# A four-block vision network on one core: results in PSUM placed by a table of banks instead of by fixed names, with new orders of the steps

## The chip, the core and the metric

The kernel runs on one core of a Trainium2 chip. A core has TensorE (PE in the profile, its weight loads PEld), VectorE (DVE), ScalarE (ACT), GpSimd (POOL) and SyncE (SP), each with its own queue of instructions that runs in order; they wait for each other through semaphores. TensorE writes its products into PSUM, which has eight banks of 128 partitions x 512 float32; VectorE and ScalarE read them there. The metric is the time of one execution on the device in microseconds (us), less is better.

## What is computed

Input x is (4, 256, 32, 32) float32: four images, 256 channels, 1024 pixels. Four residual blocks, each on the group-normalised x (32 groups of 8 channels), follow each other:

```python
x = x + _L0_conv_ref(_gn(x), ...)   
x = x + _L1_conv_ref(_gn(x), ...)
x = x + _L2_conv_ref(_gn(x), ...)
x = x + _L3_conv_ref(_gn(x), ...)
...
# L0
q = _conv1x1(x, q_w, q_b)
x_ds = lax.conv_general_dilated(x, ds_w, window_strides=(sr, sr), ...)
kv = _conv1x1(layernormed x_ds, kv_w, kv_b)
attn = jax.nn.softmax(jnp.einsum('bcm,bcn->bmn', q, k), axis=-1)
out = jnp.einsum('bmn,bcn->bcm', attn, v)
out = _conv1x1(out, proj_w, proj_b)
...
# L1
xd, z = jnp.split(xz, 2, axis=-1)
xc = jax.nn.silu(3x3 depthwise convolution of xd + cb)
delta = jax.nn.softplus(...)
h = a * h + bu          
y = layernorm(h * c + Ds * u)
out = layernorm((y * silu(z)) @ op_w, times gate and skip) @ proj_w.T + proj_b
...
# L2
attn = jnp.einsum('bnhi,bnhj->bhij', q, k) * scale
attn = jax.nn.softmax(jnp.clip(attn, -50.0, 50.0), axis=-1)
out = proj of einsum('bhij,bnhj->bhin', attn, v)
...
# L3
s = jax.nn.relu(score from the channel means, two small layers)
pools = max pooling with windows (1, 3, 5, 7, 9, 11, 13)
return frac_b * b_out + frac_s * s_out + x
```

The listing is condensed: words stand for longer expressions. L0 is attention with 8 heads of 32 channels, 1024 queries and 256 keys per image. L1 is a scan over the 1024 pixels in four directions, one for each 64 channels. L2 is attention between channels (32 x 32 for each head). L3 mixes two neighbouring sizes of max pooling for each channel.

## The kernel before

Images are counted from 0 to 3 here. The work is cut into streams, one letter each, and every stream runs over the images in turn: F (first norm, down-sampling, queries, keys and values), A (scores, softmax, weighted sums), C (first projection, second norm, layer norm, 3x3 convolution), B (gate, delta, scan, its norms, second projection), D (third norm, transposes to pixel rows, Gram matrix, channel attention, its output), M (fourth norm, scores and max pooling of images 0 and 1, summed on VectorE) and L (the same for images 2 and 3, summed on TensorE with weights on a diagonal). A stream is a Python generator for each engine; each `yield` ends a step. A string for each engine, `PE_ORDER`, `ACT_ORDER`, `DVE_ORDER`, `POOL_ORDER` and `SP_ORDER`, says whose steps come next: `F11 A33` is eleven steps of F, then 33 of A. So the order of work on each engine is fixed by hand-held tables, and nothing is decided on the chip but the waiting.

Each step has a label (`s0_0`, `mT0`, `pv0_0`, `proj1_0_0`), and raises its stream's semaphore; a reader waits for the label's number. Labels that matter below:

- A: `s{h}_{j}` (L1626) is the score of head h for a pair of query tiles; VectorE's `mx{h}_{j}` (L1071) takes the maxima of the rows. `mT{g}` (L1634) transposes the maxima, VectorE splits them in two and SyncE copies them below the queries. `st{g}_{kt}_{j}` (L1646) is the transposed score with the maximum subtracted, and ScalarE's exponential `p{g}_{kt}_{j}` (L549) reads it. `pv{g}_{kt}` (L1661) multiplies with the values and with ones; ScalarE's logarithm and exponential (L559, L562) make the inverse sums, VectorE's L1088 multiplies.
- F: `ds` (L1586), `q` (L1552 with WQ), `k` (L1606), `vT` (L1613). The keys are split in a high half (KH, ScalarE) and a low half (KL, VectorE, L1058), and SyncE (L410) and ScalarE's queue (L538) copy query and key halves into the stacks QST and KST that the scores read.
- C: `proj0` (L1552 with GA), `gn1` (L1545), `sums1` (L1573), `xd` (L1680), the convolution of nine taps.
- B: `z`, `v`, `yc` and `yv` (all L1694, four blocks of 64 x 64), `fc1`, `fc2` (the gate's small layers), `B` and `C` (L1725), `op` (L1760), `sums2` (L1573), `proj1` (L1552 with PS and WP); VectorE's `r2` (L1110) reads `proj1` and multiplies it with the norm that ScalarE has to make first (L592).
- D: `xnT` (L1770), `gram` (L1782), `rows`, `T1` (L1803), `A` (L1812), `PAT` (L1824), `WE` (L1832), `be`, `cst` (L1507), `R` (L1853), `out` (L1552 with XR and BUF).

The eight banks have names, and each kind of result has its own: `aD0`, `aD1` for scores, transposed maxima, weighted sums, first projection and half of the convolution; `aA0`, `aA1` for transposed scores, sums of C and the other half; `bA0`, `bA1` for most of B and D; `pp0`, `pp1` for F, the small layers, C chunks and the rest. Steps of one kind use the two banks by turns. Before TensorE writes into a bank, `take` lets it wait for the last reader that was noted for it:

```python
def take(self, e, slot, reader):
    if slot in self.last:
        e.wait_ge(*self.last[slot])
    self.last[slot] = reader
```

TensorE runs in order, so whatever stands behind a step that waits for a bank waits too.

## Time and profile before

| | |
|---|---|
| median of 3 runs | 857.36 us (853.52 to 858.54) |
| profiled execution, its own time | 855.84 us |
| its span, first to last instruction | 853.2 us |
| TensorE busy | 83% of the span |
| VectorE busy | 66% |
| ScalarE busy | 50% |
| GpSimd busy | 4% |
| mean granted TensorE clock | 0.895 of full |
| DMA, mean | 31 GB/s |

All later times are microseconds from the start of the span of this one execution. A row of a group of instructions gives line, engine, operation, what it writes <- what it reads with the buffers' numbers left out, shapes, the count, then the busy time of all and the mean ns of one, and after the last bar the engine's idle time just before such instructions and what ended it.
### The profile page before, as it was taken

What the parts mean: (1) busy time and instruction counts of PE and PEld (TensorE: products, weight loads), DVE (VectorE), ACT (ScalarE), POOL (GpSimd) and SP (SyncE); (2) the same over time, 40 slices, a digit from 0 to 9 for tenths busy, and PEclk for the clock granted to TensorE, in tenths of its full rate; (3) what the DMA queues carried; (4) which work ended last, traced back from release to release, by engine and by line L of the source; (5) the groups of instructions that cost most, each with busy time, mean ns of one, the idle gap of its engine ahead of it and who ended that gap; (6) DMA issues with size and microseconds to landing.
All of it is one profiled execution on the core that took longest, in us unless ns stands there. A gap on an engine that the chain in (4) does not pass through costs nothing.

```text
span 853.2 us, 9378 instructions
## 1 busy us (share of the span) xinstructions
PE 704.7 (83%) x3384; PEld 318.8 (37%) x3384; DVE 561.6 (66%) x1057; ACT 424.3 (50%) x703; POOL 32.8 (4%) x26
## 2 busy tenths in 40 slices
PE   4848986898988899999799887798597887889685
PEld 4514332243323356443333443133234452355331
DVE  3563438226829632775678888968996858876586
ACT  1202555379576557656665637576756335521211
POOL 3300002000001000000020000000200000000000
PEclk9956998799999999989889898999788669999889
DMA  7330131000131000003200000011000010000101
GB/s 265 101 93 1 50 85 58 2 1 0 51 89 54 1 2 1 1 2 85 58 1 2 1 1 2 0 56 44 0 1 1 0 50 1 0 0 1 50 0 49
DMA packets 15056, 26.87 MB, mean 31 GB/s; under 512 B 3314, under 2 KB 7058, under 8 KB 14883
## 3 DMA queue, kind: packets, MB, share of 16 engines
q1 hardware_dynamic: 11712, 22.80, 8.7%
q10 hardware_dynamic: 3298, 3.48, 1.4%
q8 instruction: 27, 0.44, 0.2%
q14 instruction: 19, 0.15, 0.1%
HBM read 14.09 MB, written 4.19 MB: 21 GB/s over the span
## 4 chain that ended last, share of the span: by engine, by line
PE 56%; DVE 22%; ACT 14%; issue 5%; SPq 1%; POOL 1%; DMA 0%; ACTq 0%; DVEq 0%; POOLq 0%
PE aD L1661 6%; PE aA L1680 4%; DVE NEGMAX L1071 4%; PE bA L1552 4%; PE aD L1680 4%; PE pp L1586 4%; PE bA L1694 3%; PE bA L1782 3%; PE aA L1646 2%; ACT PT L549 2%; PE aD L1552 2%; DVE PA_ L1398 2%; DVE HB L1393 2%; PE aD L1626 2%; PE aA L1573 2%
## 5 line engine op out<-in xcount | busy, mean ns | idle before, releaser
L549 ACT ACTIVATE PT<-aA 128x512 f32<-128x512 f32 x128 | 70.1, 593 | 85.0 <-PE aA L1646 84.5
L1071 DVE TENSOR_REDUCE NEGMAX<-aD 128x2 f32<-128x512 f32 x128 | 82.0, 684 | 24.3 <-PE aD L1626 23.0
L1626 PE MATMUL aD<-KST,QST 96*128 96x256 f16 x256 | 53.0, 312 | 25.6 <-DVE NEGMAX L1071 18.0
L1646 PE MATMUL aA<-QST,KST 98*128 98x512 f16 x128 | 45.3, 411 | 16.0 <-ACT PT L549 11.5
L1398 DVE TENSOR_TENSOR PA_<-HB 128x1024 f32<-128x1024 f32 x40 | 49.0, 1226 | 5.0 <-PE aD L1950 4.0
L1393 DVE TENSOR_TENSOR HB<-PA_ 128x1024 f32<-128x1024 f32 x40 | 48.9, 1221 | 0.6
L1626 PEld LDWEIGHTS aD<-KST,QST 96*128 96x128 f16 x256 | 19.5, 104 | 65.2 <-DVE NEGMAX L1071 38.7
L1680 PE MATMUL aA<-XNP,WTAP 64*64 64x512 f32 x288 | 37.2, 673 | 6.2 <-issue 5.7
L1552 PE MATMUL bA<-PS,WP 128*128 128x512 f32 x64 | 33.5, 663 | 9.8 <-DVE PS L1110 9.8
L880 POOL TENSOR_TENSOR GA<-GA,PT 128x1024 f32<-128x1024 f32 x8 | 19.1, 2408 | 560.3 <-ACT PT L577 560.3
L1950 PE MATMUL aD<-PA_,PT 128*128 128x512 f32 x56 | 31.2, 685 | 9.2 <-DVE PA_ L1398 5.2
L1661 PE MATMUL aD<-PT,VT 128*32 128x512 f32 x256 | 38.0, 669 | 0.8 <-DVE GV_F L975 0.8
L1661 PE MATMUL aD<-PT,ONES 128*32 128x512 f32 x256 | 35.8, 634 | 0.0
L1088 DVE TENSOR_TENSOR GA<-GA,aD 128x512 f32<-128x512 f32 x16 | 11.0, 686 | 35.9 <-ACT GA L562 30.1
L1950 PE MATMUL aA<-PA_,PT 128*128 128x512 f32 x56 | 29.5, 651 | 6.2 <-ACT PT L807 3.9
L1782 PE MATMUL bA<-SQX 128*128 128x257 f32 x128 | 32.4, 414 | 2.5 <-ACT G L623 2.5
L1646 PEld LDWEIGHTS aA<-QST,KST 98*128 98x128 f16 x128 | 11.0, 100 | 60.3 <-ACT PT L549 33.7
L1552 PE MATMUL aD<-GA,WP 128*128 128x512 f32 x64 | 29.3, 601 | 3.1 <-DVE GA L1088 2.6
L1680 PE MATMUL aD<-XNP,WTAP 64*64 64x512 f32 x288 | 31.7, 589 | 0.0
L1552 PE MATMUL pp<-XF,WQ 128*128 128x512 f32 x64 | 30.3, 600 | 1.5 <-DVE QL L1050 1.5
L1407 DVE SCALAR_TENSOR_TENSOR ACC<-PA_,COEF,ACC 128x1024 f32<-128x1024 f32 x24 | 30.8, 1281 | 0.5
L1586 PE MATMUL pp<-XF,WDS 128*128 128x256 f32 x128 | 30.6, 397 | 0.0
(303 smaller groups left out, 1374.8 us busy)
## 6 DMA issues: line engine op xcount, KB each, us to landing
XF<-in_x SPq DMA_DIRECT2D x8, 512.0 KB, 3.8
QST<-QH SPq DMA_DIRECT2D x32, 128.0 KB, 2.7
XR<-in_x SPq DMA_DIRECT2D x4, 1024.0 KB, 4.9
...
```

Of the source, the lines that this page charges most:

```text
L549: e.activation(PROB[:, 4 * kt + j, :], SLOT[f"aA{j % 2}"][:, :], ACT.Exp)\
L1071: e.tensor_reduce(NEGMAX[:, h, 2 * j:2 * j + 2], SLOT[f"aD{j % 2}"][:, :].rearrange("p (t k) -> p t k", t=2), AX.X, ALU.max, negate=True). ...
L1393: e.tensor_tensor(HB[:, 1:1 + H, :], PA4[:, cc, 1:1 + H, 0:W], PA4[:, cc, 1:1 + H, 2:2 + W], ALU.max)\
L1398: e.tensor_tensor(PA4[:, cc, 1:1 + H, 1:1 + W], HB[:, 0:H, :], HB[:, 2:2 + H, :], ALU.max)\
L1552: mm = e.matmul(s[:, :], w(cc), src[:, cc, hs(half)], start=(cc == 0), stop=(cc == CC - 1))
L1586: mm = e.matmul(s[:, m * NK:(m + 1) * NK], WDS[:, cc, n % 4, m * P:(m + 1) * P], src, start=(n == 0), stop=(n == 4 * CC - 1))
L1626: mm = e.matmul(s[:, t * NK:(t + 1) * NK], QST[0:96, h, qt * P:(qt + 1) * P], KST[0:96, h, :], start=True, stop=True)
L1646: e.matmul(s[:, :], KST[0:98, h, kt * P:(kt + 1) * P], QST[0:98, h, hs(g % 2)], start=True, stop=True)\
L1661: mm = e.matmul(SLOT[slot][HD * j:HD * j + HD, :], w, PROB[:, 4 * kt + j, :], start=(kt == 0), stop=(kt == 1))
L1680: mm = e.matmul(banks[gi][64 * half:64 * half + 64, :], WTAP[rows, cc, tap(2 * cc + gi, dy, dx), :], XNP[rows, cc, dy + 16 * half:dy + 16 ...
L1782: mm = e.matmul(s[:, 0:C + 1], XNT[:, t, m * P:(m + 1) * P], XNT[:, t, :], start=(t == 0), stop=(t == QT - 1))
L1950: mm = e.matmul(SLOT[("aA", "aD")[cc] + str(half)][:, :], DG[:, cc, k, :], PA4[:, cc, 1 + 16 * half:17 + 16 * half, 1:1 + W], start=(k == ...
```

## The change

Two things change; the computation does not.

First, the eight banks are now one list, `PSB[0]` to `PSB[7]`. For each stream a table of the source, `BANKS_A` and so on, gives the bank of each step of each image, in the order of the labels; `-` stands for a step that takes no new bank (it adds to an earlier one). A step with two results has two digits. Maker and readers look up the bank of the same label:

```diff
+class Banks:
+    def __init__(self, tensors, text, steps, first=0):
+        self.tensors, self.words, self.first = tensors, text.split(), first
+        labels = steps.split()
+        self.index, self.count = {x: n for n, x in enumerate(labels)}, len(labels)
+    def at(self, b, label, n=0):
+        return int(self.words[(b - self.first) * self.count + self.index[label]][n])
...
+BANKS_A = """
+4 5 6 7 0 1 2 3 4 5 6 7 0 1 2 3 4 6 7 0 1 2 3 4 5 6 7 0 1 2 3 4 6 57 0 1 2 3 - 0 4 1 6 2 3 7 5 4 1 6
...
-        SLOT = {n: ctx.enter_context(nc.psum_tensor(n, [P, HALF], f32))
-                for n in ("aA0", "aA1", "aD0", "aD1", "bA0", "bA1", "pp0", "pp1")}
+        PSB = [ctx.enter_context(nc.psum_tensor(f"PSB{n}", [P, HALF], f32)) for n in range(8)]
...
-            def take(b, slot, engine, label):
-
-                slots.take(e, slot, engine.at(b, label))
-                return SLOT[slot]
+            def take(st, b, step, engine, label, n=0):
+
+                k = BANKS[st].at(b, step, n)
+                slots.take(e, k, engine.at(b, label))
+                return PSB[k]
...
-                    s = take(b, f"aD{j % 2}", dve_a, f"mx{h}_{j}")
+                    s = take("A", b, f"s{h}_{j}", dve_a, f"mx{h}_{j}")
...
-                    s = take(b, f"aA{j % 2}", act_a, f"p{g}_{kt}_{j}")
+                    s = take("A", b, f"st{g}_{kt}_{j}", act_a, f"p{g}_{kt}_{j}")
```

All other uses of a bank are edited in the same way. In the setup the two small folds now lie in banks of their own, and the weighted sums take their two banks in the other order. The wait for a bank's last reader remains, but the reader is now that of the step that had the bank before by the table.

Second, the orders of TensorE, ScalarE and VectorE are new (GpSimd's and SyncE's are as they were):

```diff
 PE_ORDER = """
-F11 A33 F1 A3 F1 A3 F1 A8 F1 A3 F1 A6 F1 A2 F1 A7 F1 A5 F1 A4 C4 A4 C1 A4 C2 A2 F1 A7 C2 A2 B1 F1 B1
...
+F11 A17 F1 A30 F1 A6 F1 A9 F1 A11 F1 A1 F2 C4 F2 C1 A10 C2 A7 B1 A16 F1 A9 C2 B2 A3 B1 A2 F1 B3 A5
...
```

What stands on TensorE at three places, before and after. The first is where image 2's scores begin (L1626 before, L1690 after). PS,WP is image 0's or image 1's second projection, XNP,WTAP the convolution, XF,WDS the down-sampling, MAT,G the transposes of D. Before:

```order
L1626 MATMUL aD<-KST,QST 128x256 x4
L1552 MATMUL bA<-PS,WP 128x512 x4
L1626 MATMUL aD<-KST,QST 128x256 x4
L1545 MATMUL pp<-MV_F,MAT 128x4
L1552 MATMUL bA<-PS,WP 128x512 x4
L1680 MATMUL aA<-XNP,WTAP 64x512 x36
L1545 MATMUL pp<-MV_D,MAT 128x4
L1626 MATMUL aD<-KST,QST 128x256 x4
L1586 MATMUL pp<-XF,WDS 128x256 x16
```

After (XDS,WK and WV,XDS are image 2's keys and values, XNP,IPZ and U,WD four-block products of B, SQX Gram of D, MAT,NEGMAX the transposed maxima):

```order
L1670 MATMUL PSB<-XDS,WK 128x256 x4
L1758 MATMUL PSB<-XNP,IPZ 64x512 x4
L1677 MATMUL PSB<-WV,XDS 128x256 x4
L1758 MATMUL PSB<-XNP,IPZ 64x512 x4
L1776 MATMUL PSB<-GAPX,W1S 16x1 x2
L1782 MATMUL PSB<-HM,SMALL 128x1 x2
L1690 MATMUL PSB<-KST,QST 128x256 x32
L1847 MATMUL PSB<-SQX 128x257 x8
L1758 MATMUL PSB<-U,WD 64x512 x4
L1698 MATMUL PSB<-MAT,NEGMAX 32x128
```

The 16 pairs of scores of heads 0 to 3 (32 products) stood in pieces among other streams, and now stand in one row.

The second place is image 0's second projection, with the banks' numbers. Before:

```order
L1552 MATMUL bA0<-PS,WP1 128x512 x2
L1552 MATMUL bA1<-PS,WP1 128x512 x2
L1626 MATMUL aD1<-KST,QST 128x256 x2
L1626 MATMUL aD0<-KST,QST 128x256 x2
L1545 MATMUL pp0<-MV_F,MAT 128x4
L1552 MATMUL bA0<-PS,WP1 128x512 x2
L1552 MATMUL bA1<-PS,WP1 128x512 x2
L1680 MATMUL aA0<-XNP,WTAP 64x512 x2
```

After:

```order
L1616 MATMUL PSB3<-PS,WP1 128x512 x2
L1616 MATMUL PSB6<-PS,WP1 128x512 x2
L1616 MATMUL PSB1<-PS,WP1 128x512 x2
L1616 MATMUL PSB7<-PS,WP1 128x512 x2
L1744 MATMUL PSB2<-XNP,WTAP 64x512 x2
```

The four blocks used two banks twice and now use four, with nothing between them.

The third place is TensorE after image 3's last weighted sum. GA,WP is image 3's first projection. Before (U,MAT is a centring of B, MAT,T the rows R of D, XR,BUF the output of D):

```order
L1694 MATMUL bA<-U,MAT 64x512 x4
L1853 MATMUL pp<-MAT,T 32x128 x32
L1552 MATMUL bA<-XR,BUF 128x512 x2
L1694 MATMUL pp<-SQX,MAT 64x512 x4
L1552 MATMUL bA<-XR,BUF 128x512 x6
L1694 MATMUL pp<-SQX,MAT 64x512 x4
L1552 MATMUL aD<-GA,WP 128x512 x2
L1545 MATMUL pp<-MV_M,MAT 128x4
```

After (WP,ABD is PAT and T,W2V is WE of image 1; MV_C is `gn1`, the group norm of image 3's C):

```order
L1758 MATMUL PSB<-U,MAT 64x512 x4
L1889 MATMUL PSB<-WP,ABD 128x256 x2
L1758 MATMUL PSB<-U,MAT 64x512 x4
L1616 MATMUL PSB<-GA,WP 128x512 x2
L1897 MATMUL PSB<-T,W2V 128x256 x4
L1758 MATMUL PSB<-SQX,MAT 64x512 x4
L1616 MATMUL PSB<-GA,WP 128x512 x2
L1574 MATMUL PSB<-COL,T 128x1 x4
L1574 MATMUL PSB<-GM_D,BUF 128x1 x4
```

```order
L1616 MATMUL PSB<-PS,WP 128x512 x8
L1616 MATMUL PSB<-GA,WP 128x512 x2
L1609 MATMUL PSB<-MV_M,MAT 128x4
L1609 MATMUL PSB<-MV_C,MAT 128x4
```

One more centring and PAT, WE, be and cst of image 1 now stand behind the last weighted sum, and all of image 2's second projection stands ahead of image 3's last projection block and group norm. Before, two of its four blocks stood behind that norm.

## Rows read from the trace of the kernel before

**Rows 1.** The page: its first line, and busy time by engine
```profile
span 853.2 us, 9378 instructions
PE 704.7 (83%) x3384; PEld 318.8 (37%) x3384; DVE 561.6 (66%) x1057; ACT 424.3 (50%) x703; POOL 32.8 (4%) x26
```

**Rows 2.** Stretches: length, busy PE PEld DVE ACT POOL, clock, DMA, GB/s
```profile
417.20:559.80 142.60, 119.85 (x619) 48.58 (x618) 121.90 (x207) 84.41 (x132) 4.68 (x2) 0.88 0.00 1
559.80:803.00 243.20, 199.09 (x912) 98.57 (x910) 184.80 (x355) 116.34 (x192) 5.12 (x2) 0.87 0.05 18
803.00:853.30 50.30, 31.43 (x66) 12.24 (x66) 36.38 (x57) 7.45 (x22) 0.00 (x0) 0.85 0.05 21
```

**Rows 3.** TensorE's groups by line and shape, whole span
```profile
L1626 PE MATMUL aD<-KST,QST 96*128 96x256 f16 x256 | 53.0, 312 | 25.6 <-DVE NEGMAX L1071 18.0 <-DMA KST<-KL 5.0 <-DVE XR L1098 1.1
L1646 PE MATMUL aA<-QST,KST 98*128 98x512 f16 x128 | 45.3, 411 | 16.0 <-ACT PT L549 11.5 <-DMA QST<-ML 3.4
L1552 PE MATMUL bA<-PS,WP 128*128 128x512 f32 x64 | 33.5, 663 | 9.8 <-DVE PS L1110 9.8
L1782 PE MATMUL bA<-SQX 128*128 128x257 f32 x128 | 32.4, 414 | 2.5 <-ACT G L623 2.5
L1552 PE MATMUL pp<-XF,WQ 128*128 128x512 f32 x64 | 30.3, 600 | 1.5 <-DVE QL L1050 1.5
L1725 PE MATMUL bA<-U,XB 128*128 128x512 f32 x32 | 20.8, 775 | 3.4 <-DVE AOK L1245 1.7 <-DVE SQX L1162 1.0 <-ACT T L699 0.7
L1725 PE MATMUL pp<-U,XC 128*128 128x512 f32 x32 | 16.6, 632 | 2.3 <-DVE PS L1174 1.3 <-DVE QL L1050 1.0
L1694 PE MATMUL bA<-U,MAT 64*64 64x512 f32 x64 | 15.5, 859 | 1.2 <-DVE SQX L1162 1.2
L1634 PE MATMUL aD<-MAT,NEGMAX 128*32 128x128 f32 x8 | 2.5, 317 | 6.8 <-DVE NEGMAX L1071 6.3 <-ACT U L613 0.5
```

**Rows 4.** Timeline of image 0's second projection: start, length, engine, instruction
```profile
280.60 1.98 PE L1552 MATMUL bA<-PS,WP 128*128 128x512 f32 x4 [1.38 <-DVE PS L1110]
285.03 3.58 PE L1552 MATMUL bA<-PS,WP 128*128 128x512 f32 x4 [2.45 <-DVE PS L1110]
...
279.86 0.69 DVE L1110 TENSOR_TENSOR PS<-bA,PS 128x512 f32<-128x512 f32 x1 [2.00 <-ACT PS L592]
```

**Rows 5.** Timeline, TensorE at image 0's first and last row of scores
```profile
47.56 1.03 PE L1626 MATMUL aD<-KST,QST 96*128 96x256 f16 x4 [4.95 <-DMA KST<-KL]
...
57.70 1.02 PE L1626 MATMUL aD<-KST,QST 96*128 96x256 f16 x3
```

**Rows 6.** Groups of VectorE and ScalarE: the scores' readers
```profile
L1071 DVE TENSOR_REDUCE NEGMAX<-aD 128x2 f32<-128x512 f32 x128 | 82.0, 684 | 24.3 <-PE aD L1626 23.0
L549 ACT ACTIVATE PT<-aA 128x512 f32<-128x512 f32 x128 | 70.1, 593 | 85.0 <-PE aA L1646 84.5
```

**Rows 7.** Two stretches of image 0's attention; weighted sums at either clock
```profile
47.50:77.00 29.50, 21.21 (x75) 5.62 (x75) 21.00 (x40) 4.85 (x10) 0.00 (x0) 0.50 0.13 42
77.00:120.70 43.70, 41.63 (x233) 19.63 (x225) 13.80 (x26) 21.78 (x41) 0.00 (x0) 1.00 0.12 35
...
76.07 1.54 PE L1661 MATMUL aD<-PT,ONES 128*32 128x512 f32 x8
...
86.37 1.04 PE L1661 MATMUL aD<-PT,ONES 128*32 128x512 f32 x8
```

**Rows 8.** Timeline, SyncE's issues of query copies; DMA issues of key copies
```profile
35.62 6.10 SPq L410 DMA_DIRECT2D QST<-QH  x8
...
KST<-KL SPq DMA_DIRECT2D x16, 32.0 KB, 1.9
```

**Rows 9.** TensorE's groups by shape: small steps of D
```profile
L1832 PE MATMUL bA<-T,W2V 128*128 128x256 f32 x32 | 9.6, 453 | 1.5 <-ACT SQX L670 1.2 <-ACT GT L638 0.3
L1507 PE MATMUL bA<-GM_D,BUF 128*128 128x1 f32 x32 | 6.3, 319 | 2.4 <-ACT BUF L715 2.4
L1824 PE MATMUL bA<-WP,ABD 128*128 128x256 f32 x16 | 4.2, 384 | 1.7 <-DVE ABD L1276 1.7
```

More of the change, by code:

```diff
@@ L230, in __init__, with take @@
         self.last = {}
-    def take(self, e, slot, reader):
-        if slot in self.last:
-            e.wait_ge(*self.last[slot])
-        self.last[slot] = reader
+    def take(self, e, bank, reader):
+        if bank in self.last:
+            e.wait_ge(*self.last[bank])
+        self.last[bank] = reader
 def program(nc, x, cols, mats, wq, wk, wv, wds, wp0, small16, w1s, ipx, ipz, cw, xpr, dtp, xb, xc, opw,
@@ L1563, in sums @@
             def sums(b, l, src, ready):
[L1565 removed]
+                pe, act, dve, st, squares, _, _ = NORM["C" if l == 1 else "B"]
                 e.wait_ge(*dve.at(b, ready))
@@ L1568, in sums @@
                 for half in range(2):
-                    s = take(b, f"{banks}{half}", dve, f"ln_var{l}" if half else f"ln_var{l}_0")
+                    s = take(st, b, f"sums{l}_{half}", dve, f"ln_var{l}" if half else f"ln_var{l}_0")
                     for cc in range(CC):
@@ L1673, in convolve @@
                 e.wait_ge(*act_c.at(b, "xn1"))
-                banks = [take(b, ("aA", "aD")[cc] + str(gi), act_c, f"xd{cc}_{gi}_1") for gi in range(2)]
+                banks = [take("C", b, f"xd{cc}_{gi}", act_c, f"xd{cc}_{gi}_1") for gi in range(2)]
                 for n in range(TAPS):
@@ L1707, in small_mlp @@
                 pe, dve, hidden = (last_steps(b)[0], last_steps(b)[2], HM3) if at else (pe_b, dve_b, HM1)
-                s = take(b, "pp0", dve, f"hm{l}")
+                st = last(b) if at else "B"
+                s = take(st, b, steps[0], dve, f"hm{l}")
                 e.wait_ge(*sources)
@@ L1713, in small_mlp @@
                 yield
-                s = take(b, "pp1", dve, "sc0" if at else "gate_in")
+                s = take(st, b, steps[1], dve, "sc0" if at else "gate_in")
                 e.wait_ge(*dve.at(b, f"hm{l}"))
@@ L1787, in channel_scores @@
             def channel_scores(b):
-                s = take(b, "bA0", dve_d, "srow")
+                s = take("D", b, "rows", dve_d, "srow")
                 e.wait_ge(*dve_d.at(b, "gram1"))
@@ L1819, in attended @@
             def attended(b):
-                s = take(b, "bA1", act_d, "pat")
+                s = take("D", b, "PAT", act_d, "pat")
                 e.wait_ge(*dve_d.at(b, "abd3"))
```

327 lines of the change are left out of this document (184 added, 143 removed), and 3 rows, old and new, of the table BANKS_B.

## The prediction

> **What bounds the kernel now.** I read the page first, then the table of stretches, then the groups of instructions by shape, and last the timeline of two places. The page shows TensorE busy for 704.7 of 853.2 us, VectorE for 561.6 and ScalarE for 424.3 [rows 1]. So no engine is full; TensorE comes nearest, and its 148.5 us of idle time (853.2 - 704.7) are what an order and a choice of banks can work on.
>
> The stretches [rows 2] are cut at the first score and the last weighted sum of each image. In the last attention's stretch, 417.2 to 559.8 us, TensorE is busy for 119.85 of 142.6 us and VectorE for 121.90. From 559.8 us on, only the rest of image 1, the chains of images 2 and 3 are left: TensorE is busy for 199.1 of 243.2 us and VectorE for 184.8, and the last 50.3 us are the pooling of image 3 alone.
>
> The groups [rows 3] say who ended TensorE's idle time. I sort them by asking whether the instruction waited for its data or for a bank that somebody still had to read. Waits for a bank: scores 18.0 (L1626, on the maxima), transposed scores 11.5 (L1646, on the exponentials), second projection 9.8 (L1552, on L1110), and smaller ones: B chunks 3.4 and C chunks 2.3 (L1725), Gram 2.5 (L1782), queries 1.5 (L1552), centring 1.2 (L1694), together 10.9. The sum is 50.2 us, a third of the idle time. The rest is waits for data, as 6.3 at the transposed maxima (L1634), and would stay.
>
> **What the change removes.** The eight names of banks that each belonged to one kind of result become one pool. The maker of the score of pair j no longer needs the reader of pair j-2. Four terms follow.
>
> Second projection. At 280.60 and 285.03 us TensorE had stood for 1.38 and 2.45 us, because bA0 and bA1 were full: VectorE's L1110 had itself waited 2.00 us for ScalarE and read the first of them only at 279.86 [rows 4]. The changed table gives the four blocks four banks (3, 6, 1, 7 for image 0), so TensorE writes them all and goes on to the convolution. I take all of the 9.8 us, bounds 0 and 9.8.
>
> Small bank waits, 10.9. Counted in the tables, 328 of the 612 uses of a bank came four steps or fewer after its last use, and 48 now do. I take all 10.9, bounds 0 and 10.9.
>
> Scores, 18.0. Here the reader can be the pace and not the bank. In image 0 the 16 pairs run from 47.56 to 58.72 us, 0.70 each, and one maximum takes 0.684 [rows 5, 6]: eight banks can't make that faster. In later images VectorE was late with other work, and there a longer queue helps. I take half, 9.0, bounds 0 and 18.0.
>
> Transposed scores, 11.5. The same with ScalarE, whose exponential takes 0.593 us [rows 6]. Half, 5.8, bounds 0 and 11.5.
>
> Removed in all: 9.8 + 10.9 + 9.0 + 5.8 = 35.5 us.
>
> **What the change adds.** The new order puts the attention into blocks. All 16 pairs of images 2 and 3 stand in a row on TensorE, then one Gram product and one four-block product, then the transposed maxima.
>
> Runs of scores. One maximum is 0.684 us, so 16 take 10.9 us. At the lower clock two pairs, four records, take 1.03 us on TensorE [rows 5]; at the full clock I put 0.3 for a pair, 4.8 for 16. The first eight pairs find banks free; the other eight come at VectorE's pace, 8 x 0.684 = 5.5 against 2.4: a wait of 3 us per image, 9 for three. The second batch (eight transposed scores, eight pairs) has 5.5 us of maxima and 4.7 of exponentials against about 4.8 of TensorE: 1 us per image, 3. Of these 12 us, 6.3 stand already in the wait of L1634 [rows 3], since what ends that wait is the same maxima. Added: 5.7, bounds 0 and 12.
>
> Weighted sums of pairs 1 to 3 now have little else between them. ScalarE needs 8 x 0.593 and about 1.2 for logarithm and reciprocal, 5.9 us a pair; TensorE needs four sets of eight records of at most 1.04 us at full clock [rows 7], 4.2, plus eight transposed scores, some 2. They nearly balance. One third of a us for each of nine: 3, bounds 0 and 9.
>
> Keys. In image 0 the first score waited until 47.56 us for the copies of the low key halves, with TensorE idle for 4.95 [rows 5]. SyncE had started at 35.62, as soon as the last query half was there, and took 6.10 us to issue the eight query copies; a key copy takes 1.9 more to land [rows 8]. So 11.9 us lie between the last query and the first score. SyncE's own order is unchanged, and so is GpSimd's. But TensorE's k of image 1 now stands right before that image's scores, with only vT and one small product between, and ScalarE squares image 0's residual before it copies these keys. From image 1's last query product to its first score TensorE has four projection blocks, k and vT, about 8 us (2 each for the blocks at 33.5 / 16 [rows 3]), against the 11.9. I take 4 us open. In images 2 and 3 the queries are long done, and vT, two four-block products (at most 1.9 each) and two small layers lie behind k: 1 us each. Added: 6, bounds 0 and 12.
>
> Clock. From 47.5 to 77.0 us, where TensorE did little else than scores, its granted clock was 0.50, the lower level; from 77.0 it was 1.00, after dense work [rows 7]. At the lower level eight records of the weighted sums took 1.54 us (76.07), at the full one 1.04 (86.37). So a third of the time at the lower level is lost; a lull with the stretch behind it, some 4 us, costs 1.3. Six new lulls (two in each of images 1 to 3): 8, bounds 0 and 16.
>
> The Trainium skill speaks against this change here: its page "TensorE: Matmul & The Clock Gate", section "A second HAM failure mode: psum-queue depth-cycling", tells of a kernel that cycled through banks, idled briefly between groups and so fell back and forth between the levels. The trace shows both levels in this kernel, but not yet for that cause. The page "Perfetto Trace Analysis", section "Matmul Optimizations", advises the use of all eight banks and would let one expect only the gain, 853.2 - 35.5.
>
> Added in all: 5.7 + 3 + 6 + 8 = 22.7. The same matmuls, activations and copies run. The work before image 3's last weighted sum hardly changes: some small steps of image 1 and a centring of image 2 move behind it.
>
> **The sum.** Against the profiled execution: 853.2 - 35.5 + 22.7 = 840.4 us of span. That execution took 855.84 us, 2.6 more than its span, so 843.0. The median of the runs is 857.4, 1.5 above the profiled one; that is a fifth of a per cent and I leave it out.
>
> **Rivals.** *The waits only move.* The readers are the pace nearly everywhere: the halves of scores and transposed scores come back as nothing (-14.8) and the rest stays: 35.5 - 14.8 - 22.7 = -2.0, so 858. For it speaks image 0, where 0.70 us a pair stands against 0.684. Against it speaks that ScalarE's exponentials waited 84.5 us for TensorE in all [rows 6], so ScalarE is seldom the pace.
>
> *The full gain.* Later images' scores were held by banks alone and the lulls are filled: 50.2 recovered and 12 added give 815 of span, 818 in all.
>
> *Slower: image 3's tail starts later.* From its last weighted sum to the end lie 293.4 us in which the chain projection, norm, convolution, scan, channel attention, pooling of image 3 runs once. The new order puts on TensorE ahead of its group norm: one centring of image 2 (15.5 / 8 = 1.9), PAT, WE and cst of image 1 (4.2 / 4 = 1.1, 9.6 / 4 = 2.4, 6.3 / 4 = 1.6), and two more blocks of the second projection (33.5 / 16 = 2.1 each) [rows 3, 9]: 11.2 us. If the last weighted sum still comes at 560 and the gains of images 0 to 2 vanish in the blocks, the end moves by these 11.2 us: 867. It decides if that sum comes later than about 549. For it: TensorE's work before that point shrinks by only those first steps. Against it: in the tail TensorE is idle for 44 us (243.2 - 199.1), so part is absorbed, and 7.0 of the 11.2 have left the stretch before.
>
> *Slower: the clock.* If each attention block of images 1 to 3 runs as image 0 did until 77 us, 29.5 us at the lower level with TensorE busy for 21.2 [rows 7], a third of that is lost in each: 7.1, and with the same lost again in the second half of the block, whose loops are as sparse, 14.1; 42 for three instead of the 8 above: 877. It ends on the slow side from 10.3 us a block on. The skill's page just named would favour this one.
>
> **How the numbers follow.** Forecast (825 to 849): 0.48. Full gain (below 825): 0.11. Waits only move (849 to 866): 0.20. Later tail: 0.12. Clock: 0.09. A measurement of this kernel can tell about 1% from no change, some 8.6 us either way of 857.4. Faster is the first two, 0.59; same 0.20; slower 0.21. The range reaches from a little below the full gain, 815, to the later tail with a small margin, 870. It leaves out about 1 in 10 on each side. The likeliest case's own range is 825 to 849.
>
> **What would show it.** L1626's successor should lose most of its idle time on maxima outside the runs, and the second projection all of its 9.8. The first score of image 1 should wait for a key copy. Of the half-clock stretches there should be new ones in the attention blocks of images 1 to 3. VectorE's and ScalarE's busy times should be unchanged. The last weighted sum of image 3 should end near 549 us and the first of image 3's pooling products near 791. The forecast is wrong if TensorE's idle time doesn't fall below 140 us, or if the tail is longer than 300.

## The result and the profile after

The changed kernel takes 783.2 us at the median (781.5 to 783.7), beside 857.3 us for the kernel before. The ratio is 0.9139, with a 95% interval of 0.9112 to 0.9165: faster by 74 us, where the forecast was 14 and its range ended at 815. In a later set of runs the same kernel took 783.7 (ratio 0.9141, interval 0.9121 to 0.9161).

The page of the changed kernel, the same lines as in [rows 1]:

```profile
span 779.7 us, 9375 instructions
...
PE 664.2 (85%) x3384; PEld 313.0 (40%) x3384; DVE 555.0 (71%) x1057; ACT 418.3 (54%) x703; POOL 34.6 (4%) x26
```

The span lost 73.5 us. TensorE's idle time fell by 33.0, from 148.5 to 115.5 (779.7 - 664.2). Its busy time fell by 40.5, from 704.7, although it runs the same 3384 matmuls. VectorE's and ScalarE's fell by only 7 and 6. Any explanation has to find both halves.

TensorE's groups by line and shape in the changed kernel, as [rows 3]: busy us, mean ns of one, and the idle time before them with what ended it. The old lines 1626, 1646, 1552, 1634 and 1694 are now 1690, 1710, 1616, 1698 and 1758; the line on which VectorE reads the scores went from 1071 to 1130.

```profile
L1690 PE MATMUL PSB<-KST,QST 96*128 96x256 f16 x256 | 41.7, 310 | 12.6 <-DMA KST<-KL 7.3 <-ACT PT L607 1.3 <-DVE GA L1147 1.1
...
L1710 PE MATMUL PSB<-QST,KST 98*128 98x512 f16 x128 | 37.4, 408 | 4.7 <-ACT PT L607 1.8 <-DVE PS L1235 1.4 <-DVE AOK L1306 0.4
...
L1616 PE MATMUL PSB<-PS,WP 128*128 128x512 f32 x64 | 28.7, 599 | 0.0
...
L1758 PE MATMUL PSB<-U,MAT 64*64 64x512 f32 x64 | 15.5, 859 | 7.1 <-DVE U L1239 7.1
```

The second projection waits no more, and the scores' wait for the maxima, 18.0 us in [rows 3], is not among the first three. But look at the busy column too: the scores fell from 53.0 to 41.7 us with the mean of one record nearly the same (312 and 310). The group's busy time is the time covered by its records. Records that follow each other closely overlap; the first after a pause overlaps with nothing before it.

The changed kernel in stretches, cut where the first score of image 0 starts and where each image's last weighted sum ends, then the whole. The columns are those of [rows 2].

```profile
47.20:103.80 56.60, 48.10 (x277) 23.10 (x277) 30.64 (x60) 23.13 (x46) 0.00 (x0) 0.87 0.13 41
103.80:208.90 105.10, 88.72 (x515) 37.49 (x516) 56.41 (x102) 65.12 (x104) 4.64 (x2) 0.92 0.15 40
208.90:343.20 134.30, 128.19 (x671) 54.41 (x671) 89.37 (x180) 94.07 (x154) 4.69 (x2) 0.97 0.09 24
343.20:490.50 147.30, 142.42 (x802) 65.75 (x805) 128.19 (x242) 100.30 (x162) 6.95 (x2) 0.99 0.09 22
490.50:779.70 289.20, 226.76 (x1012) 109.72 (x1012) 230.83 (x427) 127.64 (x222) 4.66 (x2) 0.89 0.05 19
```

From 208.9 to 490.5 us TensorE idles for only 11.0 of 281.6 us, at a granted clock of 0.97 and 0.99. The last weighted sum of image 3 ends at 490.5, not at 559.8 as before: 69 of the 73.5 us are won by then. The tail is 289.2 us long, before 293.4.

The stretches at the lower of the two clock levels are fewer. These are the stretches table's closing rows for all of them together, first of the kernel before (23 stretches), then of the changed kernel (17).

```profile
sum 178.80, PE 137.59 PEld 60.63 DVE 127.81 ACT 77.40 POOL 4.65; mean PE 5.98 PEld 2.64 DVE 5.56 ACT 3.37 POOL 0.20
```

```profile
sum 110.40, PE 71.60 PEld 37.55 DVE 85.36 ACT 45.83 POOL 4.36; mean PE 4.21 PEld 2.21 DVE 5.02 ACT 2.70 POOL 0.26
```

TensorE was busy at the lower level for 137.6 us before and for 71.6 after. At that level a third of the time is lost (1.54 us against 1.04, [rows 7]), so by this estimate the clock stands for (137.6 - 71.6) / 3 = 22 of the 40.5 us of busy time.

### The profile page after: what moved, and what is told of

Read it like the earlier page. It is cut to its first block, busy times and chain, and to the rows that moved or that the text cites. A ratio compares the mean times of both kernels' runs of the same rounds, so it can differ in the third digit from the quotient of the medians.

```text
span 779.7 us, 9375 instructions
## 1 busy us (share of the span) xinstructions
PE 664.2 (85%) x3384; PEld 313.0 (40%) x3384; DVE 555.0 (71%) x1057; ACT 418.3 (54%) x703; POOL 34.6 (4%) x26
## 4 chain that ended last, share of the span: by engine, by line
PE 51%; DVE 24%; ACT 15%; issue 6%; SPq 1%; POOL 1%; DMA 1%; ACTq 0%; DVEq 0%; POOLq 0%
PE PSB L1616 11%; PE PSB L1744 6%; PE PSB L1725 5%; PE PSB L1650 3%; PE PSB L1758 3%; PE PSB L1637 3%; DVE PA_ L1459 3%; DVE NEGMAX L1130 3%; PE PSB L2015 3%; DVE HB L1454 3%; PE PSB L1710 2%; PE PSB L1690 2%; PE PSB L1825 2%; PE PSB L1574 1%; SPq L468 1%
## 5 line engine op out<-in xcount | busy, mean ns | idle before, releaser
L1130 DVE TENSOR_REDUCE NEGMAX<-PSB 128x2 f32<-128x512 f32 x128 | 78.6, 680 | 15.0 <-PE PSB L1690 14.7
L607 ACT ACTIVATE PT<-PSB 128x512 f32<-128x512 f32 x128 | 65.7, 604 | 31.1 <-PE PSB L1710 31.0
L2015 PE MATMUL PSB<-PA_,PT 128*128 128x512 f32 x112 | 58.6, 658 | 15.8 <-DVE PA_ L1459 7.0
L1744 PE MATMUL PSB<-XNP,WTAP 64*64 64x512 f32 x576 | 63.4, 591 | 0.0
L1690 PE MATMUL PSB<-KST,QST 96*128 96x256 f16 x256 | 41.7, 310 | 12.6 <-DMA KST<-KL 7.3
L1710 PE MATMUL PSB<-QST,KST 98*128 98x512 f16 x128 | 37.4, 408 | 4.7 <-ACT PT L607 1.8
L1690 PEld LDWEIGHTS PSB<-KST,QST 96*128 96x128 f16 x256 | 24.4, 110 | 32.3 <-ACT PT L607 8.2
L1725 PE MATMUL PSB<-PT,VT 128*32 128x512 f32 x256 | 34.0, 603 | 0.6 <-DVE NEGMAX L1130 0.3
L1725 PE MATMUL PSB<-PT,ONES 128*32 128x512 f32 x256 | 33.4, 592 | 0.0
L1650 PE MATMUL PSB<-XF,WDS 128*128 128x256 f32 x128 | 31.6, 406 | 0.2 <-DVE NEGMAX L1130 0.2
L1616 PE MATMUL PSB<-GA,WP 128*128 128x512 f32 x64 | 30.0, 605 | 0.0
L1847 PE MATMUL PSB<-SQX 128*128 128x257 f32 x128 | 29.6, 386 | 0.4 <-DVE NEGMAX L1130 0.4
L1616 PE MATMUL PSB<-PS,WP 128*128 128x512 f32 x64 | 28.7, 599 | 0.0
```

Source lines behind the costliest of these rows:

```text
L607: e.activation(PROB[:, 4 * kt + j, :], bank("A", b, f"st{g}_{kt}_{j}")[:, :], ACT.Exp)\
L1130: e.tensor_reduce(NEGMAX[:, h, 2 * j:2 * j + 2], bank("A", b, f"s{h}_{j}")[:, :].rearrange("p (t k) -> p t k", t=2), AX.X, ALU.max, negate ...
L1616: mm = e.matmul(s[:, :], w(cc), src[:, cc, hs(half)], start=(cc == 0), stop=(cc == CC - 1))
L1650: mm = e.matmul(s[:, m * NK:(m + 1) * NK], WDS[:, cc, n % 4, m * P:(m + 1) * P], src, start=(n == 0), stop=(n == 4 * CC - 1))
L1690: mm = e.matmul(s[:, t * NK:(t + 1) * NK], QST[0:96, h, qt * P:(qt + 1) * P], KST[0:96, h, :], start=True, stop=True)
L1710: e.matmul(s[:, :], KST[0:98, h, kt * P:(kt + 1) * P], QST[0:98, h, hs(g % 2)], start=True, stop=True)\
```

## Experiments

There are two things in the change, the free banks and the order, and 17 runs look at them. Times are medians; each set of runs had the kernel before beside it on the same chip (855.7 to 857.4), and the ratios are to that.

### Banks alone, a smaller pool, two banks for one result, another table

The first kernel has the orders of before, and a table in which each result takes the bank that was read longest ago in the trace of before:

```diff
 BANKS_A = """
-4 5 6 7 0 1 2 3 4 5 6 7 0 1 2 3 4 6 7 0 1 2 3 4 5 6 7 0 1 2 3 4 6 57 0 1 2 3 - 0 4 1 6 2 3 7 5 4 1 6
+4 5 6 7 0 1 2 3 4 5 6 7 0 1 2 3 4 5 6 7 0 1 2 3 4 5 6 7 0 1 2 3 4 67 0 1 3 4 - 0 1 3 4 2 7 6 0 3 4 2
...
 PE_ORDER = """
-F11 A17 F1 A30 F1 A6 F1 A9 F1 A11 F1 A1 F2 C4 F2 C1 A10 C2 A7 B1 A16 F1 A9 C2 B2 A3 B1 A2 F1 B3 A5
+F11 A33 F1 A3 F1 A3 F1 A8 F1 A3 F1 A6 F1 A2 F1 A7 F1 A5 F1 A4 C4 A4 C1 A4 C2 A2 F1 A7 C2 A2 B1 F1 B1
...
```

> The orders of steps of all engines are those of the kernel before; only the banks are free: each result gets, in TensorE's order, the bank that had been read longest ago in the trace of before. My new theory: most of the 74 us come from the order, which needs eight banks to run at all; then banks alone give what the prediction's terms on banks say at most, 20 to 35 us (about 825 to 837), with TensorE's idle time down by about as much and its clock (0.895) and busy time (705) nearly as before. Rival A, banks alone give the whole gain: within 10 us of 783. Rival B, the readers are the pace: above 848.

Measured: 826.4 us, ratio 0.9651 (0.9620 to 0.9682). So the banks alone give 29 us, and the order gives 43 on top of free banks. The time is neither rival's. ("Pieces" below are stretches in which TensorE is busy without a pause.) The page and the first waits of TensorE (line, what it waited for, us in total, times, longest):

```profile
span 823.6 us, 9375 instructions
...
PE 681.8 (83%) x3384; PEld 325.0 (39%) x3384; DVE 558.7 (68%) x1057; ACT 421.4 (51%) x703; POOL 32.7 (4%) x26
```

```profile
PE PSB L1698 <- DVE NEGMAX L1130: 17.2, 6, 7.0
PE PSB L1637 <- issue: 12.2, 8, 4.2
PE PSB L1609 <- DVE MV_F L1006: 11.2, 1, 11.2
PE PSB L1744 <- issue: 8.8, 2, 5.5
...
PE PSB L1710 <- ACT PT L607: 1.7, 4, 0.9
```

Here my expectation was wrong in kind, though right in size. I had expected the idle time to fall by about the gain. It fell by 6.7, from 148.5 to 141.8. Bank waits, sorted as the prediction sorted them, are down from 50.2 to about 12, but waits for data have taken their place: TensorE now stands 17.2 us at the transposed maxima, 6.3 before [rows 3], because the 16 maxima ahead of them are VectorE's pace. The 12.2 and 8.8 us that the profile puts down to "issue" (an engine that waits for nothing shown) are of that kind too: each of these ten steps starts 0.1 to 0.2 us after ScalarE has finished what it reads (those at 131.39 and 599.69 us, for example, after 131.29 and 599.59). The waits put down to "issue" are 21.0 us here, 9.8 before and 2.4 in the changed kernel. The other 22.9 us of the span's gain are busy time. I counted TensorE's pauses in both traces: 184 separate busy pieces before, 96 with free banks. At the lower level TensorE was busy for 119.0 us instead of 137.6, a third of which is 6.2 us. 16.7 us are left, and 88 restarts fewer, 0.19 us each: what a pause costs beyond its idle time, if the whole rest is put on it. The other traces bear this out roughly. A straight-line fit of busy time over the 17 traces without fillers (fillers come below) gives 0.17 us for each piece and 0.42 us, not a third, for each us busy at the lower level, and misses no trace by more than 2.5 us. In the groups, the scores went from 53.0 to 40.5 us:

```profile
L1690 PE MATMUL PSB<-KST,QST 96*128 96x256 f16 x256 | 40.5, 300 | 5.3 <-DMA KST<-KL 4.4 <-ACT PT L607 0.5 <-DVE NEGMAX L1130 0.2
```

The next three keep the changed order. One uses only banks 0 to 6. One gives the four blocks of each second projection two banks in turn:

```diff
 BANKS_B = """
-21 63 4 5 60 53 7 5 4 2 6 4 0 2 53 07 56 02 6 2 3 6 2 0 3 6 1 7 05 02 5 3 73 40 0 5 3 7 4 7 7 3 75
-40 72 16 7 4 1 6 4 3 1 6 2 5 40 47 0 2 24 57 3 7 0 3 7 5 0 7 35 40 32 60 6 0 5 4 0 5 3 4 2 0 34 20 5
+21 63 4 5 60 53 7 5 4 2 6 4 0 2 53 07 56 02 6 2 3 6 2 0 3 6 3 6 05 02 5 3 73 40 0 5 3 7 4 7 7 3 75
+40 72 16 7 4 1 6 4 3 1 6 1 6 40 47 0 2 24 57 3 7 0 3 7 5 0 7 35 40 32 60 6 0 5 4 0 5 3 4 3 4 34 20 5
...
```

The third has the table by last reading. The changed table starts as in the line with the minus, that with seven banks and that by last reading as in the two with a plus:

```diff
 BANKS_B = """
-21 63 4 5 60 53 7 5 4 2 6 4 0 2 53 07 56 02 6 2 3 6 2 0 3 6 1 7 05 02 5 3 73 40 0 5 3 7 4 7 7 3 75
+24 46 1 3 10 54 6 3 5 2 1 3 4 0 21 50 31 20 2 6 2 1 0 2 1 5 4 0 15 35 1 1 32 54 6 0 5 1 3 0 2 2 50
...
+26 21 5 5 50 74 2 7 1 3 5 2 7 6 43 70 45 76 5 6 3 5 6 7 3 5 1 0 74 76 4 3 05 23 0 5 4 7 2 4 4 3 41
...
```

> The order of the changed kernel with bank 7 never used: every result has one of seven banks. By a rough count 93 results would find their bank still full, for 42 us in sum, many of them beside other waits. My theory (the order keeps TensorE several results ahead of its readers, and its long busy stretches are what holds the clock up): 15 to 40 us slower than the changed kernel (798 to 825), idle time of TensorE up by 10 to 25 and its busy time up by 3 to 10 with a lower clock. Rival (the queue's depth does not matter beyond a few banks): within 8 us of 783.

Measured: 795.0 us, ratio 0.9279 (0.9253 to 0.9305), 12 us above the changed kernel: idle time 121.4, up 5.9, busy time 673.6, up 9.4. That is between my 15 to 40 and the rival's 8. The depth counts, less than I thought, and more of it shows as busy time than as idle time.

> The changed kernel, only the last two of the four blocks of each second projection take the banks of the first two again. The prediction's term says that this pair of waits was worth 9.8 us for four images, so 790 to 793. Rival (the wait is hidden, since VectorE is the pace there and TensorE is ahead): within 3 us of 783.

Measured: 793.4 us, ratio 0.9273 (0.9243 to 0.9302), 10 us above by the medians and 11.5 by the ratios. The prediction's term for this wait, 9.8, is about its price under this order:

```profile
L1616 PE MATMUL PSB<-PS,WP 128*128 128x512 f32 x64 | 35.1, 701 | 11.4 <-DVE PS L1169 11.4
```

The group shows 11.4 us of waiting and 6.4 more of busy time (28.7 with free banks), 17.8 in all, of which 10 to 12 reach the end.

> The order of the changed kernel, its table replaced by another one over the same eight banks, in which each result takes the bank that was read longest ago in the trace of the changed kernel. If only the number of banks counts: within 3 us of 783. If the table itself was worth something beyond that: 5 to 15 us slower.

Measured: 779.4 us, ratio 0.9092 (0.9070 to 0.9113), and in another set of runs 778.2, 0.9081 (0.9062 to 0.9100) beside 0.9141 (0.9121 to 0.9161) for the changed kernel. The plain rule is 4 to 5 us faster than the table of the change, which neither of my two cases had: the table itself brings nothing beyond its order.

The remaining corner, the changed order with the fixed banks of before, was not run, because its waits close a circle: TensorE would wait for a bank whose reader stands in its own engine's queue behind something that TensorE has yet to make. So the new order is not only helped by free banks: it can't run on the old ones.

### One kind of result freed under the old order

Here only the words of one kind change, to a bank that stands empty at that time in the trace of before; all others keep what they had. The scores of image 2 as an example (its first 25 words: sixteen pairs, the transposed maxima, eight transposed scores):

```diff
-2 3 2 3 2 3 2 3 2 3 2 3 2 3 2 3 2 0 1 0 1 0 1 0 1
+0 1 7 3 4 5 2 3 6 2 1 7 3 2 0 1 2 0 1 0 1 0 1 0 1
```

> Order of before and its fixed banks for everything but the scores: 98 of the 128 scores go to a bank other than their two, wherever one of the eight is empty at that time in the trace of before. The prediction's term for the scores was half of their 18.0 us of idle time, 9.0, so 848. Theory: a pause costs more than the idle time that the rows show, since the pair after it starts with an empty pipeline (L1626 was busy for 53.0 us in before and its successor for 40.5 with all banks free), so 10 to 18 us: 839 to 847, busy time of the scores below 46. Rival: the waits move to the transposed scores and maxima, 852 to 858.

Measured: 852.6 us, ratio 0.9956 (0.9938 to 0.9973), 3.7 us. The rival holds, with its range. The scores' wait for maxima fell from 18.0 to 4.4 us and their busy time from 53.0 to 42.6, but the waits are handed on:

```profile
L1690 PE MATMUL PSB<-KST,QST 96*128 96x256 f16 x256 | 42.6, 309 | 9.9 <-DMA KST<-KL 5.4 <-DVE NEGMAX L1130 4.4
...
L1698 PE MATMUL PSB<-MAT,NEGMAX 128*32 128x128 f32 x8 | 2.4, 298 | 14.0 <-DVE NEGMAX L1130 13.5 <-ACT U L671 0.5
```

The transposed maxima wait 14.0 us instead of 6.8: the same maxima are waited for, a few steps later. Idle and busy time of the scores' group fell by 26.1 us together (78.6 to 52.5), but TensorE's busy time as a whole only by 7.8 (704.7 to 696.9), its idle time rose by 5.2 (148.5 to 153.7), and 3.7 reached the end.

> Order of before and its fixed banks for everything but the transposed scores, 98 of 128 moved to an empty bank. Prediction's term: half of 11.5, 5.8 us, so 851. Theory: 5 to 10 us, 847 to 852. Rival: ScalarE's exponentials are the pace, below 3 us.

Measured: 854.4 us, ratio 0.9943 (0.9908 to 0.9978), 1.9 by the medians and 4.9 by the ratio. The ten runs spread from 844.5 to 857.4, so the rival (below 3) and the lower end of mine (5) are not told apart. The wait itself is only in part gone: TensorE still waited 7.4 us for the exponentials instead of 11.5.

> Order of before and its fixed banks for everything but the four blocks of each second projection, 12 of 16 moved to an empty bank. Prediction's term: all of 9.8 us, so 847. Under the order of the changed kernel the same two banks cost 10 us, so I expect 846 to 850. Rival: under the old order VectorE is late there for what follows too and the gain is below 4 us.

Measured: 857.5 us, ratio 1.0026 (1.0005 to 1.0047): no gain, if anything 1 or 2 us of loss, as the rival had it. The freed blocks do stop waiting, and the convolution behind them waits instead, for the same reader (VectorE's addition, line 1169), because they now sit in its banks:

```profile
L1744 PE MATMUL PSB<-XNP,WTAP 64*64 64x512 f32 x576 | 73.2, 665 | 13.9 <-DVE PS L1169 8.1 <-issue 5.4 <-ACT XNP L659 0.5
...
L1616 PE MATMUL PSB<-PS,WP 128*128 128x512 f32 x64 | 29.5, 601 | 0.0
```

9.8 us went from one line and 8.1 came to another. A bank that is empty is somebody's next bank as long as the others stay fixed.

> Order of before and its fixed banks for all but the scores and the transposed scores, 186 of 256 moved to an empty bank. Alone these two gave 3.7 and 1.9 us. Theory (a wait removed lets the next one in the line show; only freeing several kinds at once pays): more than the sum, 8 to 16 us, 840 to 848. Rival (the terms add up): 4 to 7 us, 849 to 852.

Measured: 850.5 us, ratio 0.9934 (0.9912 to 0.9956), 6.1 us: the terms add up, and my theory that these two need each other falls.

```profile
span 848.0 us, 9379 instructions
...
PE 691.8 (82%) x3384; PEld 325.8 (38%) x3384; DVE 559.3 (66%) x1057; ACT 422.4 (50%) x703; POOL 32.7 (4%) x26
```

TensorE's busy time is down by 12.9 us and its pieces from 184 to 119, so more than half of what free banks do for the busy time is there already. But its idle time is even higher than before, 156.2 us (848.0 - 691.8), and takes most of it back. The other 23 of the 29 us come only when all other results are free too: from here the span falls by 24.4 us, 14.4 of idle time and 10.0 of busy time. Which of the other results it takes was not tried.

### Where along the program the order pays

These kernels join the two orders, with eight banks by last reading. Up to a point in the program all engines follow one of them, then they do what is left in the sequence of the other. Below is TensorE's order for the first of them, with its junction. At a junction the steps that one order had put off come in a burst, here five of F:

```diff
...
-B1 A10 B2 A10 B2 A2 B3 C3 B1 C1 B1 F1 C1 F1 B1 F2 C1 B1 C1 B3 F1 B6 C1 D1 C1 D4 F1 B1 F1 B3 A16 D1
+B1 A10 B2 A10 B1 F5 B4 F2 B1 A2 B1 C2 B2 C2 B2 A2 B1 C1 A3 B1 C2 A2 B1 A2 B2 A2 F1 B2 C1 D1 A2 F1 D1
...
```

> All engines follow the order of the changed kernel up to the end of image 1's attention, and do what is then left in the order of before; eight banks, each result takes the one read longest ago. With the old order throughout this rule gave 826, with the new order throughout 779; the 47 us between are what is to be placed. My theory (the gain lies where images 2 and 3 get their attention in dense blocks, with TensorE's clock at the full level): little is won here, 815 to 824. Rival (the gain is made in images 0 and 1, whose attention ends 29 us earlier in the changed kernel than under the old order with eight banks): 795 to 805.

> As the run before, with the change of order at the end of image 2's attention. My theory: part of the gain, 800 to 812. Rival: all of it is there already, 779 to 795.

> As before, with the change at the end of image 3's attention: only the tail of 289 us keeps the old order. My theory: nearly all of the gain is there, 780 to 790, and TensorE's clock up to that point is that of the changed kernel (about 0.95). Rival (the tail's own order carries 10 us or more): 790 to 800. A later tail, as the prediction's rival of 11.2 us has it, would show as this run being faster than 779.

> The reverse of the first: the order of before up to the end of image 1's attention, then what is left in the order of the changed kernel. My theory: most of the 47 us is won, 785 to 795. Rival: 810 to 822.

> The order of before up to the end of image 3's attention, then what is left in the order of the changed kernel; eight banks by last reading. If the tail's order is worth its 12 us by itself: 812 to 817 (826 less 12). If it only fits its own front: 822 to 832. The prediction's later tail (11.2 us of work put ahead of image 3's chain) is not in it, since that work stands before the cut or is part of what is left.

Measured, with the ratios to the kernel before on the same chip, and the time at which TensorE had done 100, 250, 450 and all 669 us of its work. Each step is weighted with the time that it took in the run order_after_banks_by_lru, so the columns compare equal work:

| kernel | median us | ratio (95%) | at 100 | 250 | 450 | 669 |
|---|---|---|---|---|---|---|
| before | 857.3 | 1 | 143.5 | 319.5 | 561.7 | 847.5 |
| order_before_8banks | 826.4 | 0.9651 (0.9620 to 0.9682) | 137.4 | 309.9 | 541.3 | 817.8 |
| old_through_image3 | 819.7 | 0.9564 (0.9547 to 0.9581) | 139.2 | 311.9 | 540.4 | 811.9 |
| new_through_image1 | 812.4 | 0.9479 (0.9465 to 0.9493) | 127.7 | 302.4 | 529.2 | 806.4 |
| new_through_image2 | 810.2 | 0.9445 (0.9418 to 0.9472) | 126.6 | 294.5 | 521.9 | 799.1 |
| old_through_image1 | 808.6 | 0.9436 (0.9420 to 0.9451) | 141.2 | 322.2 | 528.4 | 800.6 |
| new_through_image3 | 791.2 | 0.9226 (0.9197 to 0.9256) | 127.4 | 292.3 | 509.4 | 785.5 |
| order_after_banks_by_lru | 779.4 | 0.9092 (0.9070 to 0.9113) | 128.3 | 293.9 | 500.5 | 773.0 |

My theory came out half right. The new order through image 1 won 14 us, between my 815 to 824 and the rival's 795 to 805. Through image 2 it stands at 810.2, inside my 800 to 812. Through image 3 it stands where the rival had it (790 to 800): the tail's order carries 12 us behind this front. The reverse, old through image 1, won 18 us, not most of the 47: 808.6 is nearer to the rival's 810 to 822 than to my 785 to 795. Behind the old front the new tail wins 7 by the medians, between my two cases.

The columns say why the halves don't simply add. Under the whole new order the lead over order_before_8banks is 9 us at 100, 16 at 250, 41 at 450 and 45 at the end: more than half is made between 250 and 450, which is where images 2 and 3 have their attention. old_through_image1 first falls 12 us behind at 250 (322.2 against 309.9), in the burst at its junction, and then gains 29.5 to the end. So images 2 and 3 are worth about 25 us, the first part 9 to 16, the tail 4 to 12; joining costs up to 12 and blurs the edges.

What the dense part looks like, on TensorE at image 2's first sixteen pairs (start, length, instructions, idle time before):

```profile
277.28 0.93 PE L1690 MATMUL PSB<-KST,QST 96*128 96x256 f16 x6
278.46 0.39 PE L1690 MATMUL PSB<-KST,QST 96*128 96x256 f16 x2 [0.25 <-DVE NEGMAX L1130]
279.15 2.10 PE L1690 MATMUL PSB<-KST,QST 96*128 96x256 f16 x14 [0.29 <-DVE NEGMAX L1130]
281.45 1.58 PE L1690 MATMUL PSB<-KST,QST 96*128 96x256 f16 x10 [0.21 <-DVE NEGMAX L1130]
283.24 3.74 PE L1847 MATMUL PSB<-SQX 128*128 128x257 f32 x16 [0.20 <-DVE NEGMAX L1130]
286.91 1.09 PE L1758 MATMUL PSB<-U,WD 64*64 64x512 f32 x8
287.93 0.28 PE L1698 MATMUL PSB<-MAT,NEGMAX 128*32 128x128 f32 x1
```

and VectorE in the same 16 pairs:

```profile
277.71 9.65 DVE L1130 TENSOR_REDUCE NEGMAX<-PSB 128x2 f32<-128x512 f32 x16 [0.17 <-PE PSB L1690]
287.29 0.41 DVE L1292 COPY BUF<-PSB 128x257 f32<-128x257 f32 x1
```

TensorE has written the sixteen pairs by 283.03, with some 0.8 us of waits, while VectorE reads them until 287.36. In these 4.3 us TensorE computes the Gram product and a four-block product of other images, and finds the maxima ready at 287.93. The pair alone after a pause covers 0.39 us, in the run of 14 records a pair takes 2.10 / 7 = 0.30.

Images 0 and 1 have nothing between the run and the transposed maxima, and there TensorE stands. Below are these places of image 0 and image 1, then four of the five largest waits of the changed kernel (the fifth, 14.2 us, is for the first norm):

```profile
47.19 5.97 PE L1690 MATMUL PSB<-KST,QST 96*128 96x256 f16 x32 [4.95 <-DMA KST<-KL]
57.64 0.37 PE L1698 MATMUL PSB<-MAT,NEGMAX 128*32 128x128 f32 x1 [4.48 <-DVE NEGMAX L1130]
...
135.14 0.37 PE L1698 MATMUL PSB<-MAT,NEGMAX 128*32 128x128 f32 x1 [4.47 <-DVE NEGMAX L1130]
```

```profile
PE PSB L1758 <- ACT XNP L659: 14.6, 2, 10.2
PE PSB L1698 <- DVE NEGMAX L1130: 8.9, 2, 4.5
PE PSB L1690 <- DMA KST<-KL: 7.3, 2, 5.0
PE PSB L1758 <- DVE U L1239: 7.1, 2, 5.5
```

So the new order doesn't only shorten waits, it lengthens some. For XNP it is 14.6 us, ahead of `z` of images 0 and 3 (4.4 and 10.2), against 9.3 ahead of the convolution under the old order with free banks; for the key copies 7.3 against 4.4; for U 7.1 against 3.6.

### The clock

To test the clock by itself I put matmuls that compute nothing needed into TensorE's waits, on top of the table by last reading:

```diff
+            FILL = {("s", 0): 3, ("mT", 0): 3, ("s", 1): 2, ("mT", 1): 4, ("z", 0): 4,
+                    ("gn", 3, 1): 3, ("z", 3): 9, ("yc", 3): 4, ("gn", 3, 2): 2, ("gn", 3, 3): 2, ("w1", 3): 1, ("acc", 3): 3}
+
+            def fill(s, *at):
+                for _ in range(FILL.get(at, 0)):
+                    e.matmul(s[:, :], mat("ident"), WDS[:, 0, 0:2, :].rearrange("p n c -> p (n c)"), start=True, stop=True)
...
                 s = take("A", b, f"mT{g}", dve_a, f"ml{g}")
+                if g == 0:
+                    fill(s, "mT", b)
                 e.wait_ge(*dve_a.at(b, f"mx{4 * g + 3}_3"))
```

> The order of the changed kernel with the table by last reading (779.4 us), and 40 matmuls of 128x128 by 512 that compute nothing needed, in twelve waits of TensorE that lasted 1.9 to 10.1 us: into the bank that the waiting step has just got, ahead of its wait, at most about nine tenths of each wait. They test the clock alone: in that kernel TensorE was busy for 83 us of the 124 us at the lower clock. If stretches at the lower clock cost a third of the work in them, as the prediction took it, and the filled waits keep the clock up: 765 to 775, with under 70 us at the lower level. If the work in those stretches is paced by VectorE and ScalarE anyway, or the clock falls for another reason: 777 to 785.

> The changed kernel itself, beside the two below on one chip: 781 to 785.

> The order of the changed kernel with the table by last reading. If the 4 us seen before are real: 778 to 781, else as changed_again.

> The same with 40 matmuls that compute nothing needed in twelve waits. The clock was 0.959 against 0.920 and the busy time at the lower level 56 us, fillers among it, against 83. Theory (the clock's worth here is a few us, since much of that work is paced by the readers): 2 to 5 us below after_lru_again. Rival (no gain at all): within 1 us of it.

Measured: 775.7 us (ratio 0.9052, 0.9019 to 0.9086) and, on one chip beside the others, 776.3 (0.9054, 0.9031 to 0.9078) against 778.2 (0.9081, 0.9062 to 0.9100) without the fillers and 783.7 for the changed kernel. The granted clock rose from 0.927 to 0.959. The closing rows over the stretches at the lower level, first without the fillers (16 stretches), then with them (14):

```profile
sum 114.00, PE 75.13 PEld 38.26 DVE 89.87 ACT 55.60 POOL 4.27; mean PE 4.70 PEld 2.39 DVE 5.62 ACT 3.47 POOL 0.27
```

```profile
sum 63.80, PE 56.78 PEld 28.85 DVE 47.63 ACT 31.75 POOL 0.00; mean PE 4.06 PEld 2.06 DVE 3.40 ACT 2.27 POOL 0.00
```

Fifty us less at the lower level and at least 18 us less of TensorE's work in it, of which a third is 6; the end moved by 2 to 4, and the intervals of the two overlap. So the clock is kept up by filling waits, but little of that reached the end. That the readers set the pace in much of those stretches would explain it; it isn't shown, and the fillers may also have held up steps behind them. How much of the 22 us of the account above the end of the changed kernel owes to the clock stays open.

This is also the fastest kernel of the study. The plain table alone, at 778, is 4 to 5 us better than the change; the further 2 of the fillers are not sure.

## Why the prediction was wrong

The direction was right; the size was far off, and most steps that made the size were wrong.

- **The sum of the bank waits (35.5).** Banks alone gave 29 (ratio 0.9651), so the number looks good, but not for its reasons. Term by term under the old order: scores 3.7, not 9.0; transposed scores 1.9 by the medians, not 5.8; second projection nothing, not 9.8 (under the new order it is worth its 10 us). The small waits, 10.9, were not tried by themselves. At the scores and at the second projection TensorE stopped waiting and then waited for the same reader a step or a few later. For the scores this is what the rival *the waits only move* said; the second projection it had kept whole, like the forecast. About 23 of the 29 us came only with all kinds free. In the end 22.9 of the 29.6 us of span were busy time, with half of the pauses gone: the prediction treated idle time as the whole price of a wait, and had no term for busy time except the clock's. So that 29 stands near 35.5 is luck.
- **"The rest is waits for data, and would stay."** This is the step that failed most. The prediction gave the new order no gain at all. It took 98.3 us of waits for data (148.5 - 50.2) as fixed. Freeing the banks turned most bank waits into data waits (idle 141.8), and the new order then took idle time down to 115.5, although it lengthened some waits (14.6 us for XNP against 9.3). The timeline of image 2 shows how: the wait for the maxima is filled with other images' work. The order was worth 43 us over the freed banks, 47 with the plain table. The rival *the full gain*, which had 0.11 for less than 825, missed it as well: it too counted bank waits alone, and came to 818.
- **Runs of scores (+5.7).** The picture was right, eight pairs ahead and then VectorE's pace, but not the sum. It let VectorE begin only after the first eight pairs (2.4 + 5.5 for 4.8, a wait of 3). VectorE reads from the first pair on, so image 2's sixteen pairs took 5.75 us, with 0.8 of waits. The other wait is the one for the last maxima, at the transposed maxima, and there the order listing of "The change" had shown a Gram product and a four-block product behind image 2's run. They hide it (287.93). Images 0 and 1, whose runs have nothing behind them, stand 4.5 us each there. The whole wait at L1698 is 8.9 us, against 6.8 before: 2.1 added.
- **Weighted sums (+3).** No such wait: their two groups have 0.6 us of idle time before them in all.
- **Keys (+6).** The mechanism came: the scores wait 7.3 us for key copies, 5.0 in image 0 and 2.4 in image 1, against 5.0 before. So 2.4 were added and not 6; images 2 and 3 have no such wait.
- **Clock (+8).** Wrong in sign. 110.4 us at the lower level instead of 178.8, and between 208.9 and 490.5 a clock of 0.97 to 0.99. The blocks have no more lulls than before. In image 1's the stretches at the lower level are 17.1 us long, as before; from the first score of image 2 to the last weighted sum of image 3 they shrank from 44.2 to 10.2. The Trainium skill's rule on depth-cycling ("TensorE: Matmul & The Clock Gate", "A second HAM failure mode: psum-queue depth-cycling") spoke for a loss. But it was the kernel before, with pairs of banks, whose trace shows pauses between short groups, and with eight banks and fewer pauses the granted clock rose from 0.895 to 0.904. That pauses go with a lower clock the filled waits bear out (0.927 to 0.959), at 2 to 4 us of time.
- **"All eight banks" alone.** The advice of the Trainium skill's page "Perfetto Trace Analysis" ("Matmul Optimizations") gave 29 us here by itself, under the old order, where I had let it expect 35.5.
- **The later tail (11.2 us, rival).** Too small to decide: after image 3's last weighted sum there are 289.2 us, with the old order and eight banks 284.2, so 5.0 were added. The point from which it decides, that sum later than 549, was missed by 59 us.
- **What would show it.** The scores' successor lost its waits for maxima: yes, 18.0 to 0.7. The second projection lost its 9.8: yes. Image 1's first score waits for a key copy: yes, 2.4. New stretches at the lower clock in the blocks: no, they have fewer. VectorE's and ScalarE's busy times unchanged: within 7 us. Last weighted sum of image 3 near 549: it ended at 490.5. First pooling product near 791: it came at 737.4, and the group norm ahead of it, at 803.4 before, at 729.7. Idle time under 140: 115.5. A tail over 300: 289.2. Neither rival on the slow side had support in any run.

What stays open is how the 43 us divide between less idle time (26.3 of span by the pages), the clock (15.8 by the account: (119.0 - 71.6) / 3) and the rest (1.8). The account is arithmetic on traces. Only the filled waits tested a part of it, and 2 to 4 us came back where it says 6. Nor is it shown which results had to be free for the 23 us.
